# The opening of a fused gate-and-attention kernel, written as a straight program per engine

## What is computed

```
# gate
y   = conv1d(mean(x, pixels), w_c)                    # along the 64 channels, 5 taps
yc  = sigmoid(x * y)
sa  = sigmoid(conv2d([mean(yc, channels), max(yc, channels)], w_s))   # 5 x 5
x   = yc * sa + x
# attention
xn  = groupnorm(x, 32 groups of 2 channels) * gn_w + gn_b
q, k, v = qkv_w @ xn + qkv_b                          # 4 heads of 16 channels
a   = softmax(q.T @ k / sqrt(16))                     # 256 x 256 per head and image
x   = x + proj_w @ (v @ a.T) + proj_b
```

## Time and profile before

| | |
|---|---|
| runs | 186.29, 182.51, 185.99 us |
| the profiled execution | 184.61 us; its span from first to last instruction 182.6 us |
| PE busy | 163.2 us, 89% |
| DVE busy | 136.5 us, 75% |
| ACT busy | 121.6 us, 67% |
| POOL busy | 106.3 us, 58% |
| chain that ended last | PE 77%, DVE 5%, ACT 4%, POOL 4%, issue 3%, DMA 2%, ACTq 2%, SPq 2% |

### The profile page before, as it was taken

One profiled execution on the slowest core, in us unless ns is written; L12 is line 12 of the kernel. 1 busy time (PEld: TensorE's weight loads), 2 busy tenths in 40 slices (PEclk: granted clock), 3 DMA queues, 4 the chain that ended last, 5 costly groups with the idle time before them and its releaser, 6 DMA issues.

```text
span 182.6 us, 4762 instructions
## 1 busy us (share of the span) xinstructions
PE 163.2 (89%) x1508; PEld 107.3 (59%) x1511; DVE 136.5 (75%) x280; ACT 121.6 (67%) x254; POOL 106.3 (58%) x206
## 2 busy tenths in 40 slices
PE   6988829999685999999999999999999999998791
PEld 3778428776451857666675766767575754553220
DVE  1567663677661889898998989899897978876433
ACT  3552343455682679887987988798797965758730
POOL 8926072681977267888888778888858350101110
PEclk9999955899997899999999999999999999999967
DMA  5940487516189544555464564564646465110001
GB/s 138 336 149 0 100 105 224 153 59 176 63 196 232 151 134 130 173 164 187 130 204 148 162 201 148 169 183 163 173 132 186 139 203 148 36 32 30 29 0 57
DMA packets 19296, 25.31 MB, mean 139 GB/s; under 512 B 3568, under 2 KB 16400, under 8 KB 19280
## 3 DMA queue, kind: packets, MB, share of 16 engines
q1 hardware_dynamic: 18560, 24.62, 46.2%
q10 hardware_dynamic: 720, 0.48, 1.6%
HBM read 16.22 MB, written 8.02 MB: 133 GB/s over the span
## 4 chain that ended last, share of the span: by engine, by line
PE 77%; DVE 5%; ACT 4%; POOL 4%; issue 3%; DMA 2%; ACTq 2%; SPq 2%; POOLq 0%
PE bank L794 17%; PE quad L768 16%; PE quad L780 14%; PE bank L805 7%; PE bank L824 5%; PE quad L662 5%; PE bank L815 4%; PE bank L640 2%; DMA qs<-maxrow 2%; PE bank L674 2%; ACT pt L448 2%; ACTq L217 2%; DVE negmax L608 2%; PE bank L838 1%; POOL rest L355 1%
## 5 line engine op out<-in xcount | busy, mean ns | idle before, releaser
L608 DVE TENSOR_REDUCE negmax<-quad 128x2 bf16<-128x512 f32 x128 | 83.4, 678 | 21.1 <-PE quad L768 19.4
L448 ACT ACTIVATE pt<-quad 128x512 f32<-128x512 f32 x128 | 72.8, 594 | 23.2 <-PE quad L780 23.2
L780 PE MATMUL quad<-qs,ks 97*128 97x256 bf16 x256 | 49.4, 275 | 6.7 <-ACT pt L448 3.5
L768 PE MATMUL quad<-ks,qs 96*128 96x256 bf16 x256 | 50.5, 279 | 1.2 <-DVE negmax L608 0.4
L794 PE MATMUL bank<-pt,vs 128*32 128x256 f32 x512 | 35.8, 399 | 0.0
L768 PEld LDWEIGHTS quad<-ks,qs 96*128 96x128 bf16 x256 | 21.9, 101 | 22.3 <-DVE negmax L608 13.1
L780 PEld LDWEIGHTS quad<-qs,ks 97*128 97x128 bf16 x256 | 23.8, 98 | 14.7 <-ACT pt L448 6.3
L328 POOL TENSOR_TENSOR xall<-yo,xall 128x256 f32 (+1 forms) x15 | 11.0, 731 | 31.7 <-ACT yo L472 31.7
L794 PEld LDWEIGHTS bank<-pt,vs 128*32 128x32 f32 x512 | 15.1, 112 | 12.9 <-ACT pt L448 3.3
L355 POOL TENSOR_TENSOR rest<-z,parts 128x512 f32<-128x512 f32 x15 | 17.3, 1156 | 8.0 <-issue 5.9
L805 PE MATMUL bank<-xn,wall 128*128 128x256 f32 x64 | 19.9, 397 | 0.0
(11 more groups left out here) (66 smaller groups left out, 207.7 us busy)
## 6 DMA issues: line engine op xcount, KB each, us to landing
parts_dram<-parts SPq DMA_DIRECT2D x45, 128.0 KB, 2.0
ks<-parts_dram SPq DMA_DIRECT2D x15, 192.0 KB, 3.0
qs<-parts_dram SPq DMA_DIRECT2D x15, 192.0 KB, 3.2
out<-xall SPq DMA_DIRECT2D x16, 128.0 KB, 2.1
qs<-parts_dram SPq DMA_DIRECT2D x15, 128.0 KB, 2.7
ks<-parts_dram SPq DMA_DIRECT2D x15, 128.0 KB, 2.8
xall<-x SPq DMA_DIRECT2D x3, 512.0 KB, 6.0
gate<-gate_dram SPq DMA_DIRECT2D x6, 256.0 KB, 4.1
```

The lines of the kernel that those rows point to most:

```text
L448: nc.scalar.activation(pt[:, (u + LEAD) % UNITS, :, :].rearrange("p t n -> p (t n)"), st_bank[u % 2][:, :], ACT.Exp, scale=SCALE).then_inc ...
L608: nc.vector.tensor_reduce(negmax[:, slot(1), column:column + TILES], s_bank[u % 2][:, :].rearrange("p (t n) -> p t n", t=TILES), AX.X, ALU ...
L768: mm = pe.matmul(s_bank[u % 2][:, t * N:(t + 1) * N], qs[0:KQ, slot(1), h, a, t * P:(t + 1) * P], ks[0:KQ, slot(1), h, a, :], start=True, ...
L780: mm = pe.matmul(st_bank[u % 2][:, t * N:(t + 1) * N], ks[0:KQ + 1, slot(d), h, a, t * P:(t + 1) * P], qs[0:KQ + 1, slot(d), h, a, :], sta ...
```

## The change

The turns now begin at -1 instead of -5. What stood in turns -5 to -2 becomes a list of instructions for each engine ahead of them. Pair 0's query and key product is split in two halves of 256 columns, each with its own semaphores, and its group norm runs on VectorE except for the power. Its parts go in 10 DMAs. The spatial convolution has five pieces: pairs 0 and 1, then images 4 to 7, 8 to 15 and 16 to 31. Maps 4, 5 and 6 are made in turn -1, maps 7 and 8 in turn 0; the last piece is convolved in turn 0 and its sigmoid is made of an exponential on ScalarE and an addition and a reciprocal on VectorE. ScalarE issues the DMA of the row of maxima in turns 0, 1 and 2. The table for exponentials is loaded in turn -1. Statistics of pairs 4 and 5 stand in other units. Projection and query/key product have exchanged PSUM banks. The core of the diff:

```diff
-BLOCKS = ((0, 1), (1, 2), (2, 4), (4, 8), (8, 12), (12, 16))
+BLOCKS = ((0, 1), (1, 2), (2, 4), (4, 6), (6, 8), (8, 12), (12, 16))
+ROW_ACT = 3
...
-            peeled(range(-AHEAD, LOOP_FROM))
+            peeled(range(-1, LOOP_FROM))
...
 # scalar, ahead of the turns
+            normalised(0)
+            for a in range(2):
+                act.wait_ge(z0_ready, a + 1)
+                nc.scalar.activation(parts[:, 0, 0, a * N:(a + 1) * N], z0_half[a], ACT.Identity, bias=b_qk).then_inc(first0_ready, 1)
+            for a in range(2):
+                act.wait_ge(rest0_ready, a + 1)
+                nc.scalar.copy(parts[:, 0, 1, a * N:(a + 1) * N], rest[:, a * N:(a + 1) * N]).then_inc(middle0_ready, 1)
+            chunk_gate(0, GROUP)
...
+            def group_1():
+                chunk_gate(1, 2 * GROUP)
+                channel_gate(6)
...
+            def late_gates():
+                act.wait_ge(sconv_ready, 5)
+                act.wait_ge(spread_ready, 2)
+                nc.scalar.activation(gate_s[0:4 * GROUP, 0, :], chunk_bank[2][0:4 * GROUP, 0:N], ACT.Exp, scale=-1.0).then_inc(dexp_ready, 1)
+            aside = {(-1, 2): group_1, (-1, 6): exp_table, (0, 7): late_gates}
...
                         nc.scalar.copy(maxrow[:, slot(0), :], mt_psum[0:16, :]).then_inc(mrow_ready, 1)
+                        if isinstance(k, int) and k < ROW_ACT:
+                            act.wait_ge(mrow_ready, k + 1)
+                            row_of_maxima(act, k, slot(0))
...
 # vector
+            def late_gates():
+                dve.wait_ge(dexp_ready, 1)
+                nc.vector.tensor_scalar(gate_s[0:4 * GROUP, 0, :], gate_s[0:4 * GROUP, 0, :], 1.0, None, ALU.add).then_inc(dsum_ready, 1)
+                dve.wait_ge(dsum_ready, 1)
+                nc.vector.reciprocal(gate_s[0:4 * GROUP, 0, :], gate_s[0:4 * GROUP, 0, :]).then_inc(gate_ready, 1)
+            aside = {(-1, 2): lambda: channel_maps(4), (-1, 4): lambda: channel_maps(5), (-1, 6): lambda: channel_maps(6),
+                     (0, 1): lambda: channel_maps(7), (0, 4): lambda: channel_maps(8), (0, 5): lambda: stats(4), (0, 7): lambda: group(4),
+                     (1, 0): late_gates, (1, 1): lambda: stats(5), (1, 4): lambda: group(5)}
...
+            early(0); stats(0); early_u(1); group(0); group_norm_0(); early_x(1); stats(1); channel_maps(2)
+            group(1); split_0(); proj_bias(); ysums(4); early(2); stats(2); early_u(3); group(2); early_x(3)
+            stats(3); ysums(5); group(3); channel_maps(3); ysums(6)
...
 # tensor, ahead of the turns (waits left out)
+            pair_conv(0); channel_conv(3); pair_conv(1); keep_busy(2, bank[2]); group_stats(0); transposes(2)
+            for a in range(2):
+                pe.matmul(z0_half[a], w_qk[a], xn[:, 0, :], start=True, stop=True).then_inc(z0_ready, 1)
+            group_stats(1); chunk_conv(0, GROUP, 2 * GROUP); keep_busy(2, bank[2]); spread_gate(2); spread_gate(3)
+            transposes(3); proj_bias(); channel_conv(4); queries_keys(1); group_stats(2); keep_busy(3, bank[4])
+            group_stats(3); keep_busy(3, bank[4]); channel_conv(5)
+            aside = {(-1, 1): lambda: transposes(4), (-1, 2): second_pair, (-1, 3): lambda: transposes(5), (-1, 4): lambda: chunk_conv(1, 2 * GROUP, 4 * GROUP),
+                     (-1, 5): lambda: transposes(6), (0, 0): lambda: transposes(7), (0, 2): lambda: transposes(8), (0, 6): lambda: chunk_conv(2, 4 * GROUP, IMAGES)}
...
+                    if u == 3 and isinstance(k, int) and k == 1:
+                        groupstats(4)
+                    if u == 6 and isinstance(k, int) and k == 0:
+                        groupstats(4)
+                    if u == 6 and has(5) and not late_stats:
                         groupstats(5)
-                    if u == 2 and isinstance(k, int) and k == 0:
-                        groupstats(4)
...
 # gpsimd, ahead of the turns
+            group_norm_a(1); group_norm_b(1); group_norm_a(2); group_norm_b(2); split_a(1, 1); split_b(1, 1)
...
 # sync: in turn -1 group 1's gate, in turns 1 and 2 those of groups 2 and 3
+            aside = {(-1, 1): group_1, (1, 0): lambda: late_gate_write(sp), (1, 1): lambda: gate_read(sp, 2), (2, 2): lambda: gate_read(sp, 3)}
```

More of the change, by code:

```diff
@@ L278, in turn @@
[L278 to L288, removed]
+                    stack(qs, 0, 0, 3, slot(2))
@@ L289, in turn @@
+                    stack(ks, 1, 5, 1, slot(2), part=2)
+                if has(3):
+                    wait(sp, p1_ready, k + 3)
+                    part_write(0, slot(3))
                 stands_in(aside, k, 1)
@@ L339, in turn @@
-                if has(4):
[L340 to L356, removed]
-                if has(4):
[L359 to L364, removed]
-                    nc.gpsimd.tensor_tensor(gnb[:, :], gnm[:, :], b_gn, ALU.add).then_inc(gn_shift, 1)
@@ L366, in turn @@
-                if on_pool:
-                    nc.gpsimd.tensor_scalar(parts[:, r, 1, :], rest[:, :], 1.0, 0.0, ALU.mult, ALU.add).then_inc(split_step, 1)
-                    wait(pool, st_ready, UNITS * k)
-                    wait(pool, split_step, 3 * (k + 3) + 2)
-                    nc.gpsimd.tensor_tensor(parts[:, r, 2, :], rest[:, :], parts[:, r, 1, :], ALU.subtract).then_inc(split_step, 1)
+                opening = isinstance(k, int) and k == -1
+                if has(5) and not opening:
+                    residual()
@@ L743, in _, with group_stats @@
[L743 to L746 removed]
+            def group_stats(p):
+                wait(pe, gn_stat, 2 * (p + 1))
+                wait(pe, gn_var, p)
+                pe.matmul(gs_psum[:, 0:2], groupavg, mv[:, :], start=True, stop=True)
+                mm = pe.matmul(gs_psum[:, 2:3], groupsplit, mv[:, 0:1], start=True, stop=True)
+                mm.then_inc(gs_ready, 1)
@@ L747, in _, with queries_keys @@
+            def queries_keys(p):
+                pe.wait_ge(xn_ready, p + 1)
+                wait(pe, z32_ready, p - 1)
+                for a in range(2):
+                    mm = pe.matmul(z_bank[:, a * N:(a + 1) * N], w_qk[a], xn[:, p, :], start=True, stop=True)
+                mm.then_inc(z_ready, 1)
             pe.wait_ge(band_in, 16)
@@ L862, in turn @@
                         maxt()
-                    if u == 0 and has(3) and not first_turns:
+                    if u == 0 and has(3) and not first_turn:
                         qk(1, 3)
```

451 lines of the change are left out of this document (273 added, 178 removed).

## The result

The changed kernel took 192.45 us (median of four runs, 190.88 to 194.41) against 184.99 for the kernel before; the ratio is 1.047 with a 95% interval of 1.028 to 1.067. The forecast was 186.8, range 182.2 to 190.4: the sign was right, the size was missed by 5.6 us. The profiled execution took 193.38, its span is 191.6, so 9.0 more than before. Some executions of each kernel are slower at a lower mean clock; a median called *undisturbed* leaves them out (191.53 here), and so does every ratio.

The account below looks back on a forecast made before the run. TensorE was taken to bound the kernel from turn 2 on, so turn 2's start decides; terms of -0.3, -0.8, +3.5 and -0.9 gave +1.5 us, 186.1, moved halfway towards the median's basis to 186.8, range 182.2 to 190.4.

Parts of the forecast that it names:

- later gate reads of groups 2 and 3: Gate reads needed in turns 3 and 7: cost nothing under PE's full turn, otherwise 1.3 us of SP's time each.
- this pair of costs: Turn 1: the 3.04 us wait for the row of maxima and the half clock after it, together 4.2 us, go.
- the sum: Whole kernel: -0.3 first maximum, -0.8 turn -1, +3.5 turn 0, -0.9 turn 1, together +1.5 us, giving 186.1.
- I take full clock here: Turn -1: the longer list keeps PE busier, so full clock; turn 0 starts at 37.8, 1.1 us earlier.
- the first maximum: End of the opening: DVE's first row maximum starts at 28.8 us against 29.08 before.
- VectorE's wait before the bias: Opening: DVE stands 2.5 us until PE issues the projection bias behind two gate spreads and a map transposition.
- Turn 0: forecast 14.3: Turn 0 lasts 14.3 us against 10.8, as pair 4's statistics product starts at 46.0, not 43.63.
- the chain: Turns 0 and 1: from a pair's statistics product to the next turn's first product, serial over PE, DVE, POOL, ACT; 6.10 us.
- Turn 1: forecast 11.4: Turn 1 lasts 11.4 us against 12.3: row wait gone, pair 5's statistics product 3.9 us in, then 6.1, plus 1.4.
- The reciprocal: DVE, 256 columns ahead of turn 1's first maximum: 1.4 us, bounds 0.4 and 3.8; Trainium skill estimate 2.1.
- the 0.6 in my sum: Turn 1: 0.6 us added for a clock that fell in turn 0, where PE stands some 4 us.
- The clock rival: Idle in turns 0 and 1 lowers the clock twice, costing 2.4 to 5.0 us; 188.6 to 191.2; chance 0.20.

Follow-up runs that it names:

- read3_early: The changed kernel with SyncE issuing the gate read of group 3 earlier in turn 2, right behind the first part's write; 186.24 us, ratio 1.002 to the kernel before.
- rows_by_sp: read3_early with SyncE issuing every row of maxima, as in the kernel before; 188.93 us.
- norm_first: Changed kernel, group 3's gate read early, five warm products, projection bias earlier, and GpSimd's shift before its split in turns 0 and 1; 184.02 us, ratio 0.990.
- kept_busy_again: norm_first with 14 products of zeros filling TensorE's stand in turn 0, a repeat in five rounds against the kernel before; 181.37 us, ratio 0.980.

## Why the prediction was wrong

**The step that failed: "later gate reads of groups 2 and 3 ... cost nothing while PE fills its turn; without that cover a gate read is 1.3 of SP's time."** I hid them behind TensorE, but what they delay is SyncE's next important issue, the row of maxima in turn 3, the first turn in which SyncE carries it again. It cost 4.5 us: 2.98 of wait and 1.5 of slower products at the lower clock after it. The row was issued 1.86 us after its copy and took 4.4 to land; with the gate read moved up it was 0.57 and 2.1. I had priced exactly this pair of costs at 4.2 for turn 1 and had the gate read at its 1.3, and did not ask in which turn the two would meet. read3_early shows it: 4.0 of the 4.5 go with that one edit. With the 4.5 in it, the sum would have been 191.3.

**The opening.** A second step failed in the profiled execution: "I take full clock here", and with it the full-clock prices of all that stands ahead of turn -1. Turn 0 began at 41.81 and not at 37.8: 2.8 us at the first maximum, 1.2 more in turn -1. At full clock the same code kept the forecast: in rows_by_sp the first maximum came at 28.51 (forecast 28.8), VectorE's wait before the bias was 2.41 (forecast 2.5; 4.01 in the changed kernel's profile), and turn 0 began at 36.87. How much of this the other executions of the changed kernel lost is not known.

**Right.** Turn 0: forecast 14.3, measured 14.23 (pair 4's product 7.8 us into the turn, forecast 8.2; then 6.45 for the chain, forecast 6.1); ScalarE stood 5.71 us before pair 4's normalisation, and norm_first shows that this chain bounds the turn. Turn 1: forecast 11.4, measured 11.09 (pair 5's product 5.1 us into the turn, forecast 3.9 with 1.4 added; then 5.95 for the chain); the row's wait is gone there. The reciprocal: forecast between 0.4 and 3.8, measured 1.74. That is 0.3 to 0.4 from either value: the 1.4, which the sum in the prediction gives as 1.34, and the 2.1 of the estimate from the Trainium skill ("VectorE: DVE Perf Modes", "First, the fixed hardware budget"). The clock fell after turn 0's stand, 0.50 from 56 to 58; keeping PE busy there gave more than the 0.6 in my sum (1.5 in turns 0 and 1 of kept_busy_again). The clock rival had two falls. The first, after turn 0's stand, came; the second, in turn 1, did not come in this execution. Two others came in the opening, from 17 and from 24, and one in turn 3, which the rival did not have. So its 188.6 to 191.2 was near the result in part by luck.

**Open.** Why the clock falls in one execution and not in another of the same code, after the same idle time: in the opening after 1.57 us, in turn 1 after 1.32. The longer turn 1 of four profiles goes with this second fall, but no run takes it apart.

## What to carry to other kernels

When an issue is moved from one queue to another for some turns only, follow the first turn in which the old queue has it again, and everything else that was moved to that queue. Look at two numbers, how late the issue is and how long it takes to land: here a large read ahead of a small row went with both. A queue's work is hidden only as long as nothing urgent stands behind it. A stand of TensorE costs its length and then the slower products after it, so a chain that can't be shortened is worth filling, if the fill is shorter than the stand at the lower clock too. Before an edit is credited with a gain, compare profiles at the same granted clock, and from a common event rather than from zero.

## What was unexpected

- ScalarE pays for a DMA issue: 0.53 us each, and the turn of 7.95 became 0.45 or more longer, though ScalarE was busy for only 6.8 of it.
- The addition on 16 x 256 took VectorE 0.76 us while GpSimd ran the gate of pair 6 beside it, and 0.28 in norm_first, where GpSimd's came later (0.76 in all seven profiles with the two side by side, 0.28 in all three without):

```profile
55.39 0.72 POOL L413 TENSOR_TENSOR ycall<-ycall,gate 128x256 f32<-128x256 f32 x1
...
55.50 0.76 DVE L644 TENSOR_SCALAR gate_s<-gate_s 16x256 f32<-16x256 f32 x1 [4.43 <-ACT gate_s L509]
56.29 1.74 DVE L646 RECIPROCAL gate_s<-gate_s 16x256 f32<-16x256 f32 x1
```
```profile
49.12 0.28 DVE L647 TENSOR_SCALAR gate_s<-gate_s 16x256 f32<-16x256 f32 x1 [3.30 <-ACT gate_s L512]
```
